# Overlapping the turns of the attention core: the next turn's first scores ahead of the last products with v, and its first two exponentials ahead of the copy

## What is computed

```python
qkv = lax.conv_general_dilated(qkv, w_dw, ..., feature_group_count=3 * c) + b_dw[None, :, None, None]
q, k, v = jnp.split(qkv, 3, axis=1)
q = _l2norm(q, axis=2)
k = _l2norm(k, axis=2)
attn = jnp.einsum('bhdn,bhdm->bhnm', q, k) * temperature[None]
attn = jax.nn.softmax(attn, axis=-1)
out = jnp.einsum('bhnm,bhdm->bhdn', attn, v)
out = jnp.einsum('bchw,oc->bohw', out.reshape(b, c, h, w), w_proj) + b_proj[None, :, None, None]
```

## Time and profile before

| what | us |
|---|---|
| median of three runs | 15135.77 |
| these runs | 15133.83 to 15137.4 |
| the profiled execution | 15134.94 |
| its span, first to last instruction | 15133.0 |
| TensorE busy in it | 13078.2 (86%) |
| VectorE busy | 12834.2 (85%) |
| ScalarE busy | 11086.5 (73%) |
| GpSimd busy | 10521.8 (70%) |

### The profile page before, as it was taken

The page is one execution under the profiler, slowest core; times in us unless marked ns, Lnnn a source line. Parts: engine busy times, 40 slices in busy tenths (PEclk is TensorE's granted clock), DMA queues, the critical chain, the costliest instruction groups (busy, mean ns, idle before and its releaser), DMA issues.

```text
span 15133.0 us, 238522 instructions
## 1 busy us (share of the span) xinstructions
PE 13078.2 (86%) x61176; PEld 7845.4 (52%) x61176; DVE 12834.2 (85%) x13813; ACT 11086.5 (73%) x22762; POOL 10521.8 (70%) x4198
## 2 busy tenths in 40 slices
PE   6888988889888898888988889888898888988889
PEld 4555455554555545555455554555545555455554
DVE  8999669996799957998589985899849998499984
ACT  5887578875788757886678866788667886678866
POOL 5998069980699707997079970899608996099950
PEclk9999999999999999999999999999999999999999
DMA  3433023430344303443034420334203442033420
GB/s 111 130 129 118 20 94 127 132 107 20 98 129 137 97 20 102 130 136 92 20 109 130 137 85 20 117 127 136 80 20 121 131 134 75 20 128 129 135 68 25
DMA packets 907944, 1467.97 MB, mean 97 GB/s; under 512 B 38912, under 2 KB 891904, under 8 KB 893664
## 3 DMA queue, kind: packets, MB, share of 16 engines
q1 hardware_dynamic: 906560, 1452.37, 30.1%
HBM read 1350.07 MB, written 102.17 MB: 96 GB/s over the span
## 4 chain that ended last, share of the span: by engine, by line
PE 30%; issue 22%; POOL 21%; DVE 17%; ACT 5%; DMA 4%; DVEq 1%; POOLq 0%; ACTq 0%; SPq 0%
POOL area L1526 15%; DVE area L1042 12%; PE ps L864 9%; PE ps L878 8%; POOL area L1536 5%; PE ps L662 4%; DVE area L1060 3%; DMA area<-bc_rows 3%; ACT ps L1326 1%; PE ps L592 1%; PE ps L737 1%; PE ps L649 1%; PE ps L760 1%; POOL area L1515 1%; ACT ps L1287 1%
## 5 line engine op out<-in xcount | busy, mean ns | idle before, releaser
L1042 DVE TENSOR_TENSOR_SCAN area<-ps,hst,area 128x384 f32<-128x384 f32 x9216 | 8593.1, 1006 | 115.1 <-POOL area L1526 52.9
L1526 POOL TENSOR_TENSOR area<-area 128x1152 f32<-128x1152 f32 x3072 | 8004.9, 2642 | 50.3 <-POOL area L1515 39.3
L1326 ACT ACTIVATE ps<-area,a_neg 128x384 f32<-128x384 f32 x9216 | 5290.1, 580 | 1154.8 <-DVE area L1042 1093.3
L662 PE MATMUL ps<-area,ident 128*128 128x384 f32 x12672 | 4596.5, 499 | 804.0 <-POOL area L1536 737.5
L662 PEld LDWEIGHTS ps<-area,ident 128*128 128x128 f32 x12672 | 2275.8, 193 | 2518.5 <-POOL area L1536 960.1
L649 PE MATMUL ps<-ident,area 128*128 128x128 f32 x17280 | 2422.1, 277 | 6.0 <-ACT area L1295 6.0
L1510 POOL TENSOR_TENSOR area<-area,ones 128x2304 f32<-128x2304 f32 x8 | 43.4, 5421 | 3365.4 <-ACT area L1251 3245.1
L1469 ACT ACTIVATE area<-ps,t_neg,area 128x768 f32<-128x768 f32 x1728 | 1617.8, 986 | 918.1 <-PE ps L864 918.1
L649 PEld LDWEIGHTS ps<-ident,area 128*128 128x128 f32 x17280 | 2193.9, 193 | 60.1 <-ACT area L1295 10.9
L1536 POOL TENSOR_TENSOR area<-area 128x1152 f32<-128x1152 f32 x768 | 2027.2, 2640 | 34.8 <-ACT hst L1271 34.8
L1295 ACT ACTIVATE area<-ps,area 128x384 f32<-128x384 f32 x2880 | 1637.1, 568 | 541.2 <-PE ps L640 539.5
(11 more groups left out here) (132 smaller groups left out, 9720.1 us busy)
## 6 DMA issues: line engine op xcount, KB each, us to landing
area<-bc_rows SPq DMA_DIRECT2D x1536, 768.0 KB, 6.7
xz<-x_normed SPq DMA_DIRECT2D x144, 288.0 KB, 6.3
area<-in_x SPq DMA_DIRECT2D x18, 1728.0 KB, 10.5
area<-x_padded SPq DMA_DIRECT2D x24, 1250.0 KB, 5.5
z_raw<-z_st SPq DMA_DIRECT2D x144, 192.0 KB, 6.2
area<-z_raw SPq DMA_DIRECT2D x8, 3456.0 KB, 15.1
x_padded<-x_st SPq DMA_DIRECT2D x120, 200.0 KB, 7.7
x_normed<-area SPq DMA_DIRECT2D x9, 1728.0 KB, 7.9
```

The source lines that it names most:

```text
L662: m = e.matmul(ps[:, 5 + j, 0:CH], ident[:], hb[:, i % NH, j], start=i == 0, stop=i == N - 1)
L1042: e.tensor_tensor_scan(rev(hb[:, i % NH, j], k), rev(ps[:, 2 + j, 0:CH], k), rev(dbu[:, i % NH, j], k), hst[:, i, j:j + 1], ALU.mult, ALU. ...
L1326: e.activation(ps[:, 2 + j, 0:CH], dlt[:, par, j], ACT.Exp, scale=a_neg[:, j, k, i:i + 1]).then_inc(da, 1)
L1526: e.tensor_tensor(dbu[:, i % NH], du[:, par], row_b[:, q % 2, i % ROWS:i % ROWS + 1].broadcast_to([128, J, CH]), ALU.mult).then_inc(dbus, 1)
```

## The change

On TensorE `scores` and `values` take the turn c as well, and the six register values of a pair are made ahead of its first turn. `scores(0)` of turn c + 1 is put where turn c has no scores, between `values(33)` and `values(34)`; only turn 0 of a pair still starts with its own `scores(0)`. On ScalarE the copy of turn c stands behind the exponentials w = 0 and w = 1 of turn c + 1; for the third turn it stays at the end. No instruction on data is added or removed, and which semaphore is waited for, and with which value, is the same for each of them.

```diff
@@ TensorE, attention(b), for p in range(PAIRS) @@
                     alone(e)
+                    turns = [e.snap(b * 6 + (c + 3 * p)) for c in range(3)]
+                    bases = [e.snap(turn * 36) for turn in turns]
+
+                    def scores(c, m):
+
+                        e.wait_ge(ex, bases[c] + (2 * m + 2))
+                        for s in range(2):
+                            for h in range(2):
...
+
+                    def values(c, w):
+                        m, h = divmod(w, 2)
+                        e.wait_ge(ex, bases[c] + (w + 4))
+                        if w == 0:
+                            e.wait_ge(o_ev, turns[c] + 1)
...
+
+                    scores(0, 0)
                     for c in range(3):
-                        turn = e.snap(b * 6 + (c + 3 * p))
-                        base = e.snap(turn * 36)
...
-                        scores(0)
                         for m in range(MT):
                             if m + 1 < MT:
-                                scores(m + 1)
-                            values(2 * m)
-                            values(2 * m + 1)
+                                scores(c, m + 1)
+                            elif c < 2:
+                                scores(c + 1, 0)
+                            values(c, 2 * m)
+                            values(c, 2 * m + 1)
@@ ScalarE, attention(b), for p in range(PAIRS) @@
                     alone(e)
-                    for c in range(3):
-                        turn = e.snap(b * 6 + (c + 3 * p))
-                        base = e.snap(turn * 36)
+                    def copy_out(c, base):
+
+                        e.wait_ge(pv, base + (2 * MT + 4))
+                        e.activation(q_v[:, p, ds(c * QC, QC)].rearrange("p (s l) -> p s l", s=2),
+                                     ps[:, 6:8, 0:CH], ACT.Copy).then_inc(o_ev, 1)
+
+                    bases = [e.snap((b * 6 + (c + 3 * p)) * 36) for c in range(3)]
+                    for c, base in enumerate(bases):
                         for w in range(2 * MT):
                             m, h = divmod(w, 2)
+                            if c and w == 2:
+                                copy_out(c - 1, bases[c - 1])
                             e.wait_ge(s_mm, base + (w + 1))
                             e.wait_ge(pv, base + (w + 1))
                             e.activation(pb[:, w % 4].rearrange("p (s l) -> p s l", s=2),
...
-                        e.wait_ge(pv, base + (2 * MT + 4))
-                        e.activation(q_v[:, p, ds(c * QC, QC)].rearrange("p (s l) -> p s l", s=2),
-                                     ps[:, 6:8, 0:CH], ACT.Copy).then_inc(o_ev, 1)
+                    copy_out(2, bases[2])
```

More of the change, by code:

```diff
@@ new lines, in attention @@
+                    turns = [e.snap(b * 6 + (c + 3 * p)) for c in range(3)]
[4 more added lines that the diff above has]
+                            for h in range(2):
+                                rows = slice(64 * h, 64 * h + 64)
+                                i = e.matmul(ps[:, 2 * ((2 * m + h) % 3) + s, 0:CH], kz[rows, p, m * 128:(m + 1) * 128],
+                                             q_v[rows, p, c * QC + s * CH:c * QC + (s + 1) * CH], start=True, stop=True)
+                                if s == 1:
+                                    i.then_inc(s_mm, 1)
@@ new lines, in values @@
+                    def values(c, w):
[3 more added lines that the diff above has]
+                            e.wait_ge(o_ev, turns[c] + 1)
+                            if p == 1 and c == 0:
+                                alone(e)
+                                e.wait_ge(on, b * 12 + 6)
+                        for s in range(2):
+                            i = e.matmul(ps[64 * h:64 * h + 64, 6 + s, 0:CH], vt[:, p, m, 64 * h:64 * h + 64],
+                                         pb[:, w % 4, s * CH:(s + 1) * CH], start=m == 0, stop=m == MT - 1)
+                        i.then_inc(pv, 1)
```

## The result

The changed kernel takes 15081.62 us (median; 15078.4 to 15084.51) against 15133.83 for the kernel before in the same comparison: a ratio of 0.9965 with a 95% interval of 0.9956 to 0.9974, 52 us or 0.35% faster. The forecast was 15083. The profiled execution took 15081.83 with a span of 15079.7.

A forecast was written before the change was run, and what follows sets the result against it. The prediction took TensorE alone to bound the attention core. 55.0 us from boundaries less 3 for registers gave 52 off 15134.94, so 15083 us; likeliest case 15075 to 15091, wider range 15070 to 15100.

The forecast's parts named there:

- The bound: In the attention core TensorE alone sets the time; whatever shortens a turn shortens the image, and nothing else is next.
- (1) The boundary as an ordinary step: At 32 of 48 turn boundaries, scores slipped between products make an ordinary step: 1.72 us each, 55.0 us gained.
- (2) The changes of shape: TensorE's switches between scores and products at a boundary rise from three to five; 0.36 us per two, already in the 55.0.
- The rival of dear changes: A switch of matmul shape on TensorE costs 0.49 us instead of 0.18: 20 us, 15103 us; chance 0.03.
- (3) The copy: ScalarE's copy behind two exponentials is covered by 0.15 to 0.24 us; cost 0 to 8 us, taken as nothing.
- the rival of the late copy: New turn's first product waits for ScalarE's copy, heads may fall out of step: 8 to 26 us, 15091 to 15109; chance 0.12.
- (4) The register values: Four more TensorE register instructions before pair 0's first scores cost 0.4 us, eight times: 3 us lost; bounds 0 to 6.
- The rival of registers in every wait: Six values not kept in registers add instructions to each wait, lengthening 864 steps: 15204 us; chance 0.02.
- (5) The granted clock: Slow second steps at pair 0's start, 1.9 to 2.7 us each, may shift: 7 us more to 12 less, taken as 0.
- The sum of 52 us: Total gain over the kernel: 55.0 us from the boundaries less 3 us for register instructions.

The follow-up runs named there:

- the second trace of the changed kernel: The changed kernel, with nothing edited, profiled once more; 15080.85 us.

## Why the prediction was right

**The bound.** TensorE alone in the core: right. What the boundaries lost less came out one to one in the core: the core of pair 1, up to the products w = 32 of its third turn, went from 160.34 us to 156.92 in seven of eight images, 3.42 = 2 x 1.71 us. No other engine or DMA took over there.

**(1) The boundary as an ordinary step**: right, and to the size. 55.0 us were taken, 54.7 is what the traces have. Both parts are seen: 17.5 us less busy time on L877 (32 x 0.56 = 18) and 34.3 less idle time on L863 (32 x 1.07). The rest of the 54.7 is the 0.08 by which the wait is longer from start to start (1.15) than the idle time that the profile gives (1.07). The 0.56 is what the late exponential costs against two ordinary groups, each of which has its changes of shape in it.

**(2) The changes of shape**: right. The five changes at a boundary cost what they cost in a step: 5.88 us are two steps of 2.94. The rival of dear changes is out. That the 0.36 us a step come from the changes was only worked out; the old boundary bears it out, since there w = 34 follows w = 32 without a change, and its first matmul starts 0.32 us behind the last (1686.74, 1687.06), where the scores after a change start 0.43 behind (1683.80, 1684.23). The Trainium skill (TensorEngine Tiling (Array Packing), Key Properties) says that a change of tiling mode drains TensorE. The trace fits that, with nothing beyond the 0.36 us a step.

**(3) The copy**: right in its value (nothing), but by 0.02 us. The cover was put at 0.15 to 0.24 us from the copy's end, and it is 0.26; but 0.14 of that goes to a wait and a weight load and 0.11 to the second head, which leaves 0.02. What the rival of the late copy feared, two heads out of step, is there twice in 32 in the changed kernel's own trace, both in the same image, though not by a late copy. The timeline there:

```profile
13076.30 0.98 PEld L877 LDWEIGHTS ps<-area 128*64 128x64 f32 x8 [0.55 <-issue]
13076.31 1.65 PE L877 MATMUL ps<-area 128*64 128x384 f32 x8
```

1.65 in place of 1.52: the second head started 0.15 behind the first in place of 0.01, with the copy's end 0.26 us ahead, as at the other boundaries. At an ordinary boundary the register instruction between the heads runs ahead of the first weight load; here it runs between the two. Why it is late now and then, no run shows. It cost 0.13 us once and 0.05 once.

**(4) The register values**: too dear, the one term that was wrong. 3 us were taken for four more instructions at each start of pair 0. The chain of the changed kernel there is

```profile
1634.33 0.39 issue
1634.72 2.98 PE ps L863 x8
```

with the same 0.39 as in the earlier trace rows. The premise was off: the trace has no instruction at the lines of the `snap`s, in either kernel. The register instructions of TensorE stand at the waits, 864 at those of the scores in both kernels, and between the release and the first scores there is one before and after. So nothing was moved ahead of the first scores. The count of all recorded instructions is the same too, 238522. The rival of registers in every wait is out by this and by the step of 2.938 us, which did not change.

**(5) The granted clock**: right that it costs or gives some us either way. In the changed kernel's trace four of eight first turns have a slow second step, in the first of before five, in the second trace of the changed kernel seven, in that of before four; each costs 1.9 to 2.7 us.

The sum of 52 us held, the size within 0.5 us, and that close it is partly luck. The boundaries gave 54.7, and the 3 us for the registers don't exist. Between the two profiled executions, which are 53.3 us apart, other terms cancel: the granted clock gave 3 us more in the first turns and 5 between the pairs, while the scan stretches took 8 and the time ahead of the first scores 1.5.

## To carry to other kernels

At the boundary of two loops that are each well overlapped, look for the engine order that leaves out one member of the alternation; the next loop's first block can stand there, if each of its waits is met when its turn comes. Write down for each engine what its list has next when the moved work is ready: here each half of the change alone puts a wait ahead of something that was free before and loses a few us by the traces, while both together win 0.35%. And a hidden instruction should be priced with its cover down to hundredths of a us, since the next edit that adds to it pays in full.

## What the runs showed of the hardware

- The stretch between the two pairs has two lengths in one and the same execution, and they go with the granted clock. From the products w = 32 of pair 0 to the first scores of pair 1 it takes 26.12 us in some images and 23.45 to 23.62 in others, in both kernels. The windows of the changed kernel (length, PE, PEld, DVE, ACT, POOL, PEclk):

```profile
1797.00:1819.00 22.00, 19.64 (x80) 13.35 (x78) 8.81 (x15) 17.88 (x38) 0.00 (x0) 0.77 0.52 184
...
5529.00:5551.00 22.00, 18.99 (x92) 11.98 (x89) 8.71 (x16) 18.77 (x39) 0.00 (x0) 0.92 0.48 162
```

  At the same place of the image the granted clock has a mean of 0.77 in the first image and 0.92 in the third. In ten such windows of four kernels 0.77 goes with the long kind each time and 0.92 with the short one. What decides between the two is not shown. One such stretch is worth 2.5 to 2.7 us and a slow second step 1.9 to 2.7, eight of each in an execution, so they can account for much of the 5 to 20 us by which single executions of one kernel scatter; the traces, boundary by boundary, tell these kernels apart better than their medians do.
- The products of the two heads, in different halves of the array, run side by side even when one head starts late. With 0.37 us between the starts the pair takes 1.91 us in place of 1.52, and in the kernel before, with 0.69 between them, it takes 2.19; one behind the other would be 2.7 or more, an estimate from eight starts 0.32 us apart.
- From the end of an exponential to the scores that wait for it, it is 0.04 us. From the end of a late copy to the product, which has two waits, it is 0.14, and the other head, behind a register instruction, starts 0.11 later.
